# A state-space loop on one core: y products ahead of the output products, skip and gate ahead of the additions out of PSUM

## The reference, cut to what matters

```python
proj = hidden_states @ in_proj_w.T
gate, xBC, dt = jnp.split(proj, [INTER, INTER + CONV_DIM], axis=-1)
# conv: depthwise causal convolution of xBC over 4 tokens, + conv_b
x, Bm, Cm = jnp.split(silu(conv), [INTER, INTER + NG * SS], axis=-1)
scores = jnp.einsum('bclhn,bcshn->bchls', Cc, Bc) * Lmat      # Lmat = tril(exp(cs_l - cs_s))
Ydiag = jnp.einsum('bchls,bcshp->bclhp', scores, xdt)
Yoff = jnp.einsum('bclhn,bchpn,bchl->bclhp', Cc, prev, jnp.exp(cs))
Y = Ydiag + Yoff + x * D                     # the y products, and the skip
yg = Y * silu(gate)                          # the gate
# rstd: of the mean square of yg in each of 8 groups of 1024 channels
out = (yg * rstd) * norm_w @ out_proj_w.T    # summed over 8192 channels
```

## Time and profile before

| | |
|---|---|
| time, median of 3 runs | 2223.58 us (2219.56 to 2225.03) |
| the profiled run | 2223.88 us, of it the profile's span 2222.1 us |
| state-space loop, read at 560 to 2005 us of the span | 1445 us |
| busy in the span: PE, DVE, ACT, POOL | 2141.8 (96%), 1660.0 (75%), 1434.2 (65%), 1031.9 (46%) us |
| DVE's six taps of a step, one of them | 0.74 us |
| an output product (6 matrix products) | some 1.4 us |

### The profile page before, as it was taken

The page is one execution under the profiler, slowest core; times in us unless marked ns, Lnnn a source line. Parts: engine busy times, 40 slices in busy tenths (PEclk is TensorE's granted clock), DMA queues, the critical chain, the costliest instruction groups (busy, mean ns, idle before and its releaser), DMA issues.

```text
span 2222.1 us, 34801 instructions
## 1 busy us (share of the span) xinstructions
PE 2141.8 (96%) x12604; PEld 1750.1 (79%) x12604; DVE 1660.0 (75%) x2661; ACT 1434.2 (65%) x3090; POOL 1031.9 (46%) x755
## 2 busy tenths in 40 slices
PE   7989889999999999999999999999999999998999
PEld 7866678887788878878878887887887888787887
DVE  7777673225888898899889889889888988987121
ACT  4488643335978767668776776767867677683332
POOL 5577445352354345344454434534445443454442
PEclk9999999999999999999999999999999999999999
DMA  3000012331432323233224232323322432231332
GB/s 133 1 1 2 1 44 86 95 93 54 153 131 102 110 95 109 94 120 117 93 86 142 94 117 86 109 99 115 124 86 86 143 106 104 86 110 48 95 95 81
DMA packets 65337, 202.53 MB, mean 91 GB/s; under 512 B 7056, under 2 KB 9104, under 8 KB 56976
## 3 DMA queue, kind: packets, MB, share of 16 engines
q1 hardware_dynamic: 65168, 200.31, 26.6%
HBM read 197.39 MB, written 2.88 MB: 90 GB/s over the span
## 4 chain that ended last, share of the span: by engine, by line
PE 74%; DVE 12%; ACT 8%; issue 4%; DMA 1%; POOL 0%; SPq 0%; DVEq 0%; ACTq 0%; POOLq 0%
PE ps L1678 70%; ACT eb L899 2%; DVE x L1469 2%; DVE eb L1439 2%; PE ps L1982 2%; PE ps L1800 2%; DVE work L1393 1%; DMA eb<-scr_decays 1%; PE ps L1693 1%; DVE PT L1305 1%; ACT eb L906 1%; DVE eb L1432 1%; DVE yTl L1461 1%; DVE xdt L1411 1%; DVE nm L1283 1%
## 5 line engine op out<-in xcount | busy, mean ns | idle before, releaser
L551 POOL TENSOR_TENSOR wAl<-rawA,wAh 128x512 fp32r<-128x512 f32 x233 | 324.3, 1404 | 399.2 <-ACT wAh L691 398.7
L1678 PE MATMUL ps<-xTh,wAh 128*128 128x512 f32 x1512 | 426.4, 403 | 8.9 <-DVE work L1393 3.2
L1678 PE MATMUL ps<-xTl,wAh 128*128 128x512 f32 x1512 | 415.2, 396 | 0.0
L1678 PE MATMUL ps<-xTh,wAl 128*128 128x512 f32 x1512 | 415.2, 396 | 0.0
L1393 DVE SCALAR_TENSOR_TENSOR work<-ps,chp,work 128x510 f32<-128x510 f32 (+2 forms) x465 | 343.5, 744 | 45.7 <-ACT work L862 35.7
L1678 PEld LDWEIGHTS ps<-xTh,wAl 128*128 128x128 f32 x1512 | 284.7, 188 | 69.6
L1678 PEld LDWEIGHTS ps<-xTh,wAh 128*128 128x128 f32 x1512 | 275.9, 189 | 80.2 <-issue 20.1
L1678 PEld LDWEIGHTS ps<-xTl,wAh 128*128 128x128 f32 x1512 | 284.4, 188 | 69.4
L557 POOL TENSOR_TENSOR wBl<-rawB,wBh 128x512 fp32r<-128x512 f32 x108 | 141.6, 1324 | 386.0 <-ACT wBh L695 386.0
L899 ACT ACTIVATE eb<-eb,gc 128x128 f32<-128x128 f32 x1008 | 307.7, 392 | 12.9 <-DMA eb<-scr_decays 12.9
L601 POOL TENSOR_TENSOR sqt<-gt 128x512 f32<-128x512 f32 x110 | 152.4, 1385 | 116.7 <-DVE gt L1455 108.2
(11 more groups left out here) (208 smaller groups left out, 3979.0 us busy)
## 6 DMA issues: line engine op xcount, KB each, us to landing
eb<-scr_decays SPq DMA_DIRECT2D x62, 1536.0 KB, 6.4
rawA<-ma_in SPq DMA_DIRECT2D x144, 256.0 KB, 3.6
rawA<-fa_in SPq DMA_DIRECT2D x88, 256.0 KB, 2.6
rawB<-mb_in SPq DMA_DIRECT2D x64, 256.0 KB, 2.9
rawB<-fb_in SPq DMA_DIRECT2D x44, 256.0 KB, 2.6
x<-x_in SPq DMA_DIRECT2D x8, 256.0 KB, 6.4
x_out<-x SPq DMA_DIRECT2D x8, 256.0 KB, 2.7
wqraw<-wqkv_in SPq DMA_DIRECT2D x1, 1536.0 KB, 11.4
```

The source lines that it names most:

```text
L551: nc.gpsimd.tensor_tensor(wAl[:, slot, :], rawA[:, slot, :], wAh[:, slot, :].bitcast(F32), ALU.subtract).then_inc(A_lo, 1)
L1678: return nc.tensor.matmul(o, l, r, start=start, stop=end, **kw)
```

## The change

In the PE's step the two calls of `y_products` stand ahead of the output products of tiles 4 to 7, and no longer behind them. In the DVE's step all four `evacuate` (tiles 4 to 7), and in v = 0 `mean_square`, stand behind the second gate; before, the one of tile 4 stood inside the second group of taps, after its first tap, and the other three ahead of skip. No instruction is added or removed, and no semaphore value changes.

```diff
@@ DVE, step(v, g)
             taps(gn, conv[0])
-            taps(gn, conv[1], (1,))
-            if drain:
-                evacuate(*before, 4)
-            taps(gn, conv[1], (2, 3))
-            if drain:
-                for t in range(5, NT):
-                    evacuate(*before, t)
-                if v == 0:
-                    mean_square(g - 1, 4)
+            taps(gn, conv[1])
             ending = last and v == TPG - 2
             ...
             gate(g, v, 0)
             skip(g, v, 1)
             gate(g, v, 1)
+            if drain:
+                for t in range(4, NT):
+                    evacuate(*before, t)
+                if v == 0:
+                    mean_square(g - 1, 4)
@@ PE, step(v, g)
             chunk(gn, todo[0])
             chunk(gn, todo[1])
+            y_products(v, g, 0)
+            y_products(v, g, 1)
             if v % 2 == 0 and not first:
                 vp, gp = (v - 1, g) if v else (TPG - 1, g - 1)
                 out_products(vp, gp, 1)
                 if v == 0:
                     sum_squares(gp, 4)
-            y_products(v, g, 0)
-            y_products(v, g, 1)
```

## The result

| | before | after |
|---|---|---|
| median of 4 runs each, on one chip | 2223.34 us | 2256.86 us (2255.6 to 2258.45) |
| the profiled run | 2223.88 us, span 2222.1 us | 2255.6 us, span 2253.8 us |

The ratio is 1.0156, with an interval from 1.0141 to 1.0171: the changed kernel is 33.5 us slower. The forecast was +27.9 us, 2251, with a range of 2234 to 2265.

What follows compares the result with a forecast made beforehand. PE was taken to set the pace, busy 1417.4 of 1445 us in the state-space loop. The terms 16.0 + 5.0 + 0.3 + 2.8 - 1.5 + 5.3 gave +27.9 us on 2223.88: 2251, range 2234 to 2265.

Steps and rivals of the forecast that it cites:

- v = 2, the wait: Before tile 7 in seven groups, PE waits 4.21 us for tile 4's copy instead of 1.93: +16.0 us.
- The clock: Behind tile 7 of v = 2, half clock falls once in all seven groups instead of four: +5.3 us, bounds 0 and +17.
- What was given back: Waits for decay terms in step v = 3 of three late groups go, as DVE runs ahead: -1.5 us.
- v = 4 and 6: Plain-addition steps: PE waits 0.31 us at tile 7 where it had no wait; 16 steps, +5.0 us.
- + 3.05: DVE's time from the start of the first skip to the first instruction behind the second gate, 3.05 us.
- The last drain step: v = 6 of the last group, priced like the other plain steps, at a 0.31 us wait.
- v = 0: PE waits 0.4 us for tile 4's evacuation in seven steps: +2.8 us.
- Priced at nothing: Decay terms for the moved y products in v = 2, and SP's loads issued 4 to 5 us later: 0.
- the signs: Profile after: PE's evacuation waits near 33 us instead of 16.6, update some 1.8 us, waits for y products (L1446) gone.
- The waits are smaller: Rival: POOL does not delay the update, short waits vanish, clock falls no more often: +10 to +15, 2236; chance 0.14.
- more is lost: Rival: clock low twice in each group (+12 over the sum), or decay terms late (+3.5): 2265; chance 0.11.
- Faster: Rival: y products put ahead cover tile 4's evacuation, so the stall at tile 7 disappears: 2202; chance 0.06.

Runs made afterwards that it cites:

- experiment 2: The changed kernel with tile 4's evacuation right behind the six taps and ahead of the first skip, in all drain steps: 2216.9 us, ratio 0.9971.
- experiment 8: Kernel before, with only v = 2 of the seven later groups changed, tile 4 evacuated right behind the six taps, tiles 5 to 7 behind the gates: 2203.9 us.
- v2_only: Kernel before, with the full change in step v = 2 of the seven later groups only: 2240.9 us, ratio 1.0083.
- v0_only: Kernel before, with the full change in step v = 0 of the seven later groups only: 2222.9 us, ratio 1.0007.
- last_only: Kernel before, with the full change in the loop's last drain step only (v = 6 of the last group): 2226.8 us, ratio 1.0022.
- v46_only: Kernel before, with the full change in steps v = 4 and 6 only, without the loop's last drain step: 2231.0 us, ratio 1.0035.

## Why the prediction was right, point by point

**The bound, and the place.** PE sets the pace, and the long stall is at tile 7 of v = 2: the changed kernel's waits show it, and so do experiment 2 against the changed kernel and experiment 8 against v2_only, in which moving one evacuation returns 40 and 37 us.

**v = 2, the wait.** Right in every term on DVE's side:

| | forecast | measured |
|---|---|---|
| six taps | 4.43 | 4.44 |
| skip to update | 3.05 | 3.05 |
| update beside POOL | 1.77 | 1.78 to the copy |
| copy to PE's restart | 0.75 | 0.74 |
| PE's wait, from start to start | 4.21 | 4.14 |
| of it more than before | 2.28 | 2.09 |

The last line is a slip of the working: 4.21 counts from start to start, and from it the 1.93 us of a bracket were subtracted. Counted alike, from tile 4's first product to tile 7's, it is 6.21 us before and 8.30 after, and 4.10 in a step without a wait (not 4.16). So the wait makes 14.6 us in seven groups and not 16.0.

The rule of the Trainium skill (SBUF — State Buffer, section "Who interferes with whom") holds: with POOL away the update falls to 0.74 us, and the plain additions out of PSUM run at 0.69 us or less each beside POOL.

**The clock.** Right that it falls in all seven groups, and nearly right in size. I had taken 1.77 us for each fall; in the kernel before, v = 2 takes 17.75 us with a fall and 16.16 without, 1.59, so four falls were 6.4 us. In the changed kernel I take the time from tile 7's first product to the first of the two chunks ahead of the next drain step: 28.54 us in the first group's v = 2, where the clock stays up, 30.04 to 30.09 in four of the seven groups, and 29.82, 31.00 and 29.88 in the three later ones. These are 11.2 us over, 4.8 more than before, against the +5.3 of the forecast. It is close by misses that cancel: a fall costs less than 1.77, it costs least (1.3 us) where it begins in the wait, which had been named as a bound, and one was double, which belonged to a rival.

**What was given back.** Too small: 3.0 us and not 1.5. Before, the time from the end of v = 2's drain step to those two chunks was 27.3 us in four groups and 27.9 in three, where a step without a wait has 27.1; after the change nothing of that is left but what the low clock costs. The first y products of v = 3 had started 0.59 us late in three groups (0.50 to 0.53 in the bracket), and the output products of v = 3 had taken some 0.2 us longer in all seven. The second part had not been seen.

The v = 2 and v = 4 rows of the table, less a plain step's cost in v = 4 (7 x 0.57), are 15.6 + 4.8 - 4.0 = 16.4 us, and 14.6 + 4.8 - 3.0 is 16.4. The forecast had 16.0 + 5.3 - 1.5 = 19.8.

**v = 4 and 6.** Right that there is a small wait, the size missed: 0.57 us a step, 8.6 in fifteen, not 0.31. The term that was too small is "+ 3.05". Its row was of a step in which POOL disturbs the second gate only. In v = 4, POOL is at its weights (L551, until 1408.40) already at the first:

```profile
1405.86 2.54 POOL L551 TENSOR_TENSOR wAl<-rawA,wAh 128x512 fp32r<-128x512 f32 x2
...
1407.25 0.74 DVE L1446 SCALAR_TENSOR_TENSOR xc<-xc,chp,ps 128x512 f32<-128x512 f32 x1
1408.02 0.92 DVE L1455 TENSOR_TENSOR gt<-xc,gt 128x512 f32<-128x512 f32 x1
...
1410.54 1.87 DVE L1484 TENSOR_TENSOR oacc<-ps,oacc 128x512 f32<-128x512 f32 x3
```

Skip to evacuation is 3.29 us, the first gate takes 0.92 where it takes 0.69 alone, and PE, ready at 1403.90 + 6.93 = 1410.83, restarts at 1411.27:

```profile
1411.27 0.73 PE L1675 MATMUL ps<-wBh,yTh 128*128 128x512 f32 x2 [0.21 <-DVE oacc L1484]
1411.84 0.62 PE L1675 MATMUL ps<-wBl,yTh 128*128 128x512 f32 x2
```

That is 0.44 us between starts, of which the bracket shows 0.21, and another 0.1 us is in the first two products after a wait, whose successors start 0.57 later instead of the usual 0.46.

**The last drain step.** The failed step of the working is the word "16 steps": I priced this one like the others, though the code puts `decay_off` ahead of skip there, and the change moves tile 4 past it as well. It costs 4.8 us in the step, and 4.9 by itself on the chip, where I had 0.31. It is the largest miss, and in the opposite direction to the clock's.

**v = 0.** 2.1 us against 2.8; alone it can't be told from nothing.

**Priced at nothing, and the signs.** The moved y products do not wait for decay terms in v = 2 (no such wait in the trace there), and nobody waits for SP's later loads. DVE's waits for y products (L1446) are gone, from 21.6 to 1.4 us. PE's waits for evacuations are 37.9 us (30.6 and 7.3) where the signs named some 33; 3.6 of the difference is the last drain step's.

**The rivals.** "The waits are smaller" fell with the update's 1.74 us and the 0.57 of plain steps; "more is lost" needed two low stretches in each group, and one group had them (four in v2_only). "Faster" named its own deciding point, tile 4's copy by the time PE is at tile 7. DVE was too late for it by the 4.2 us that the rows gave; experiment 8 meets it by the order of two pieces of work, and gives 2203.9 where the rival had 2202.

The mechanism and the place were right; that the total is this close is luck, a sum of misses with both signs: 27.9 - 3.4 (v = 2: 1.4 in the wait, 0.5 in the clock, 1.5 given back) + 3.9 (fifteen plain steps) + 4.5 - 0.5 (the last step, and behind the loop) - 0.7 (v = 0) + 0.1 (the first v = 2) = 31.8, where the two profiled runs lie 31.7 apart; the medians lie 33.5 apart, since the profiled run of after is 1.3 us below its median.

## What to carry to other kernels

When a consumer is moved behind other work on an in-order engine, look at which buffer it frees and for whom: of four evacuations only the first had an output product waiting for its bank in the same step, and it alone had to stay ahead of the skips and gates, while the other three were rightly moved behind them. Price a short wait by the difference of two starts and not by its bracket (0.21 us in the bracket, 0.44 between starts, 0.57 in the step), and go through every variant of the code that the moved line passes (the first, the last, the one with an update), since one step with two more instructions on the way cost as much as eight plain ones. An order that is right in the steps with a stall need not be applied in those without: seven steps gave the whole gain here, and applying it to all 31 gave 13 us of it back.

## What the runs showed of the hardware

The granted clock fell without a wait that would explain it: behind sixteen one-column product instructions that stood directly ahead of a chunk (PE idle for 0.14 us ahead of them, then busy 2.00 of 2.00 us), for 3.4 us, in four of seven groups of experiment 2, and in none of v0_only or of the changed kernel, where the same order stands. With a wait of 1.93 us it fell in four of seven groups of the kernel before and of last_only, and in three of v46_only and v0_only. With 3.9 us it fell in all seven, once for 6.8 us in the changed kernel and four times in v2_only, up to 1.9 us before PE's restart. A fall of 3.4 us behind the restart cost about 1.6 us (17.75 against 16.16).

A VectorE instruction with two operands in SBUF beside GpSimd took 1.74 instead of 0.74 us (the update), 0.92 to 0.97 instead of 0.69 (a gate) and, as a pair of decay terms beside the weight split, 3.42 instead of 1.28 us; starting GpSimd's squares 2.8 us later in seven steps, with no other change, made the kernel 15 us faster.
